# A decoder stack on one core: in the ternary stage ScalarE scales and shifts the last four weight chunks, and VectorE clips them after its last chunk of z

## The reference, cut to what matters

```
scale = 1.0 / clip(mean(|w|), 1e-5)                 # one number for a whole weight
wq    = clip(round(w * scale), -1, 1) / scale
gate  = act_quant(x) @ wq_gate.T ;  up = act_quant(x) @ wq_up.T
inter = silu(gate) * up                             # 2048 wide, called z in the kernel
out   = act_quant(fwht(inter)) @ wq_down.T          # fwht: Walsh-Hadamard over 2048
x     = layernorm(x + out)
```

## Time and profile before

| | us |
|---|---|
| median of 3 runs | 1766.6 |
| lowest and highest of them | 1761.59, 1771.72 |
| the profiled execution's own time | 1760.69 |
| its span, from the first to the last instruction | 1758.8 |

### The profile page before, as it was taken

The page is one execution under the profiler, slowest core; times in us unless marked ns, Lnnn a source line. Parts: engine busy times, 40 slices in busy tenths (PEclk is TensorE's granted clock), DMA queues, the critical chain, the costliest instruction groups (busy, mean ns, idle before and its releaser), DMA issues. The chain is left out here.

```text
span 1758.8 us, 26394 instructions
## 1 busy us (share of the span) xinstructions
PE 1591.5 (90%) x8780; PEld 1121.4 (64%) x8812; DVE 1296.5 (74%) x2354; ACT 936.4 (53%) x1932; POOL 690.9 (39%) x646
## 2 busy tenths in 40 slices
PE   7999998999867899999889999999898989999995
PEld 5788875555525556566666566565566767677774
DVE  6466656666888899997687585784849999767574
ACT  3221226776665566666566465473634555555542
POOL 5034265776522332323332222322132235555553
PEclk9999999999988999999999999999999999999998
DMA  6200018533020000003312121121233100000000
GB/s 213 75 1 24 1 49 234 173 97 97 26 96 1 1 1 1 1 1 104 89 55 73 37 73 55 55 73 37 86 99 93 46 10 1 1 25 12 13 24 24
DMA packets 66849, 95.72 MB, mean 54 GB/s; under 512 B 12176, under 2 KB 28688, under 8 KB 66716
## 3 DMA queue, kind: packets, MB, share of 16 engines
q1 hardware_dynamic: 58460, 80.40, 15.0%
q0 software_dynamic: 6144, 12.60, 2.8%
q10 hardware_dynamic: 2112, 1.05, 0.2%
HBM read 56.25 MB, written 4.19 MB: 34 GB/s over the span
## 5 line engine op out<-in xcount | busy, mean ns | idle before, releaser
L2948 PE MATMUL bank<-fp_xT,fp_weights_values 128*128 128x512 f32 x704 | 187.1, 404 | 11.6 <-DVE fp_gate L2851 9.8
L1783 ACT ACTIVATE causal_probs<-bank,causal_neg 128x512 f32<-128x512 f32 (+3 forms) x256 | 134.1, 530 | 106.0 <-DVE causal_neg L1853 70.8
L2948 PEld LDWEIGHTS bank<-fp_xT,fp_weights_values 128*128 128x128 f32 x704 | 129.7, 190 | 57.1 <-DVE fp_gate L2851 18.0
L2975 PE MATMUL bank<-fp_wd,fp_hT 128*128 128x512 f32 x528 | 133.8, 394 | 4.6 <-DVE X L2873 3.4
L2860 DVE SCALAR_TENSOR_TENSOR fp_up<-bank,fp_weights_scales,fp_up 128x512 f32<-128x512 f32 x132 | 99.1, 751 | 44.5 <-ACT fp_up L2758 37.0
L820 DVE TENSOR_REDUCE heads_neg<-bank 128x1 f32<-128x512 f32 x128 | 86.7, 679 | 57.7 <-PE bank L869 57.6
L782 ACT ACTIVATE heads_probs<-bank,heads_neg 128x512 f32<-128x512 f32 x128 | 88.1, 689 | 77.1 <-DVE heads_neg L820 77.1
L1126 POOL DMA_DIRECT2D causal_qS<-causal_qk x96 | 48.4, 511 | 202.3 <-DVE causal_qk L1118 202.2
L1185 POOL TENSOR_TENSOR ternary_z<-ternary_z 128x1024 f32<-128x1024 f32 x16 | 37.7, 2354 | 206.1 <-DVE ternary_z L1376 206.1
L2975 PEld LDWEIGHTS bank<-fp_wd,fp_hT 128*128 128x128 f32 x528 | 98.5, 188 | 28.9 <-issue 6.6
L1511 PE MATMUL bank<-weights_raw,ternary_qT 128*128 128x512 bf16 x433 | 104.7, 388 | 4.6 <-DVE ternary_z L1376 2.6
(11 more groups left out here) (266 smaller groups left out, 4128.2 us busy)
## 6 DMA issues: line engine op xcount, KB each, us to landing
pairs_xd<-X SPq DMA_DIRECT2D x64, 128.0 KB, 2.7
pairs_cd<-in_ctx SPq DMA_DIRECT2D x64, 128.0 KB, 2.8
causal_qS<-causal_qk SPq DMA_DIRECT2D x96, 64.0 KB, 2.8
causal_qS<-causal_qk POOLq DMA_DIRECT2D x96, 64.0 KB, 2.5
causal_kS<-causal_qk SPq DMA_DIRECT2D x96, 64.0 KB, 2.7
causal_kS<-causal_qk POOLq DMA_DIRECT2D x96, 64.0 KB, 2.5
X<-in_x SPq DMA_DIRECT2D x4, 1024.0 KB, 7.8
heads_cT<-in_ctxT SPq DMA_DIRECT2D x4, 1024.0 KB, 6.1
```

The costliest lines, as they stand in the source:

```text
L1783: act.activation(probs_of(i)[:, h + one], view[:, one], ACT.Exp, bias=neg[:, G % 2, at:at + 1], accum_out=total[:, G % 2, at:at + 1]).then ...
L2948: last = pe.matmul(banks[4 + g][:], values[:, g, n % NI, of], xT[:, part, g], start=part == 0, stop=part == 1)
L2975: last = pe.matmul(banks[t][:], hT[:, n % SLOTS, a, t * P:(t + 1) * P], wd[:, c, i], start=i == 0 and k == 0, stop=i == NI - 1 and k == 2)
```

## The change

In steps 2 and 3 the shift of the two chunks moves from VectorE's queue to ScalarE's. It is a new helper, `shift_by_act`, which does the same arithmetic, from the chunk to the same place, in one ScalarE instruction: the rate is its scale operand (one number per partition) and ROUND its bias. ScalarE issues it behind silus(t, 3) and ahead of `keep_q`, with a wait for the rate and one for the shift before it. VectorE's `round_weights` becomes `clip` alone, and this stands behind z_chunk(t, 3) instead of ahead of it. Chunks 0 to 7, all other steps, all transfers and all sizes stay.

```diff
+    def shift_by_act(self, act, n):
+        act.wait_ge(self.rated, 2)
+        act.wait_ge(self.shifted, n)
+        act.activation(self.chunks[n], self.chunks[n], ACT.Copy, scale=self.rate[:, n // 4:n // 4 + 1],
+                       bias=ROUND).then_inc(self.shifted, 1)
@@ ScalarE's step
                 silus(t, 3)
+                if t in (2, 3):
+                    for n in (2 * t + 4, 2 * t + 5):
+                        weights.shift_by_act(act, n)
                 if tile(t + 1) and t >= 0:
@@ VectorE's step
                     weights.means(dve, slice(2, 3), banks[4][:, 0:1], 2)
+                z_chunk(t, 3)
                 if t in (2, 3):
                     for n in (2 * t + 4, 2 * t + 5):
-                        round_weights(n)
-                z_chunk(t, 3)
+                        weights.clip(dve, n)
                 peaks(t - 2)
```

## The result

| | before | changed |
|---|---|---|
| median us (20 runs each) | 1765.78 | 1775.58 |
| lowest run | 1760.74 | 1767.37 |
| ratio to before, 95% interval | | 1.0039 [1.0023, 1.0055] |
| span of the profiled execution, us | 1758.8 | 1777.3 |
| from z(2,2) to the first z of step 4 in it | 584.33 - 539.08 = 45.25 | 591.28 - 539.62 = 51.66 |

z(2,2), VectorE's third z of tile 2, starts at 539.08 and 539.62, ahead of all that the change touches; these 0.5 us arose ahead of the stage (a matching instruction stands at 300.21 and 300.68 already). One run of each twenty (1868.62 and 1862.83) was in a slower state; it counts in the medians and not in the ratio. So steps 2 and 3 cost **6.4 us** more, where +3.3 was forecast, and in these two profiles the part behind the stage took another 10.9 us more.

A forecast was written before the change was run, and what follows sets the result against it. Bound: shift_y(0)'s start in step 2 and the last keep in step 3. Terms: +2.1 (step 2) + 1.2 (step 3) + 0 (clock) = +3.3 us on the median 1766.6, giving 1769.9; range 1761 to 1777.

The forecast's parts named there:

- What bounds the steps: Steps 2 and 3: shift_y(0)'s start sets the end of step 2, the last keep that of step 3.
- ScalarE's queue: Step 2: two ScalarE shifts of 2.00 us and the keeps behind them make shift_y 1.58 us late by ScalarE's queue.
- The clips beside GpSimd: Step 2: clips meeting GpSimd's butterflies cost 1.23 to 1.88 us each, 1.88 taken; step 2 +2.1 us.
- Step 3: Last keep ends at 576.42 instead of 575.19, +1.2 us; clip contention hidden by 0.4 us.
- The clock: TensorE's granted clock in steps 2 and 3: -2.1 to +2.8 us, taken as 0.
- Behind step 3 nobody idles, so it is carried to the end: Behind step 3: the +3.3 us from steps 2 and 3 reaches the end of the kernel unchanged.
- Table loads: Rival, steps 2 and 3: ScalarE's added instruction costs four table loads of 1.28 us; +8.4 us, 1775.0; chance 0.03.
- VectorE decides and the shifts vanish: Rival, steps 2 and 3: VectorE's work decides and its shifts simply vanish; -5.2 us, 1761.4; chance 0.06.
- The slower rival: Steps 2 and 3: ScalarE's queue becomes the whole path, down(0) at the lower clock; +10.2 us, 1776.8; chance 0.07.
- "Same" and not "slower": Whole kernel: a measurement tells some 0.5%, 9 us, from no change; same 0.91, slower 0.07, faster 0.02.

The follow-up runs named there:

- e3: Changed kernel with GpSimd's butterflies in steps 2 and 3 waiting until both clips are done; median 1764.7 us, ratio to before 0.9994.
- e2: Changed kernel with VectorE's clips ahead of z_chunk(t, 3) again, ScalarE still shifting; median 1766.5 us, ratio to before 1.0007.
- e7: Kernel before plus a pure delay: VectorE reduces y(0) once more, into an unused place, ahead of its peaks; median 1765.4 us, ratio 0.9994.
- e8: Kernel before with step 3's rounding moved ahead of z of the third chunk, ScalarE's two keeps ahead of keep_q; median 1765.8 us, ratio 0.9985.
- e11: The same version as e8, run again against the kernel before; median 1763.6 us, ratio 0.9997.
- e9: Changed kernel plus one 128x512 VectorE reduce, 0.6 us, into an unused place ahead of peaks(0); median 1769.8 us, ratio to before 1.0032.
- e4: The changed kernel again without an edit; median 1774.9 us, ratio to before 1.0047.
- e12: The changed kernel a third time without an edit; median 1770.0 us, ratio to before 1.0047.
- e5: Changed kernel with GpSimd's two butterfly instructions of tiles 2 and 3 cut into four each; median 1764.9 us, ratio to before 0.9996.

## Why the prediction was right in its range and short in its main term

The measured 1775.6 lies in the stated 1761 to 1777, but only by the widening for the spread of runs: the terms' own bounds ended at +6.1 us and 1773, and both the +6.4 at the steps and the median lie over them. In that the hit is luck.

- **What bounds the steps: right.** shift_y(0)'s start and the last keep of step 3 set the two ends. In the changed kernel the same two moved, and step 4 with them.
- **ScalarE's queue: right.** Two shifts took 4.09 and 4.08 us for 4.04 worked out. Without contention shift_y would come 1.58 late by the sum; in e3, where only that is left, step 2 came out 1.63 us longer (from z(2,2) to the first z of step 3, 18.75 against 17.12).
- **The clips beside GpSimd: the term that was mis-sized.** The step was "so a clip costs 1.23 to 1.88, and I take 1.88, since the row above is just this meeting". The meeting was the right one, the bound was not: in rows 8 and 9 the VectorE instruction asked at 457.24, behind the start of a GpSimd instruction that ran only to 456.76 + 1.28 = 458.04. It ended at 459.12, 1.08 behind that end, and in the changed kernel the two clips of step 2 end 1.08 and 1.09 behind GpSimd's ends. Another meeting in the trace of before has the same distance at another price:

```profile
464.68 1.59 DVE L615 TENSOR_SCALAR weights_raw<-weights_raw 128x2048 f32<-128x2048 f32 x1
```

```profile
462.65 2.53 POOL L663 TENSOR_TENSOR pairs_cL<-pairs_cd,pairs_cH 128x1024 fp32r<-128x1024 f32 x1
```

  The clip ends at 466.27, 1.09 us behind GpSimd's 465.18, and took 1.59 because it asked only 0.50 us before that end. GpSimd's instructions in steps 2 and 3 are 2.36 long, so what is left of one can be 2.3. The 1.88 was read as a slowdown of the clip, bounded by itself, when it was the remainder of the other's instruction and 1.1 us more. Measured: 2.57 and 3.37. Step 2 cost 4.1 instead of 2.1.
- **Step 3: the same error, and a cover that went.** "Clip 11 starts at 572.20 and ends by 574.08 even at 1.88, ahead of keep 11, so the contention is hidden by 0.4 us here." With 5.87 us for both, keep 11 waited 1.38 us for it and ended 2.75 us later, counted from SiLU(3,3) (582.03 - 571.62 against 575.19 - 567.53), where 1.2 was forecast. TensorE gave 0.5 back ahead of that SiLU and took 0.1 behind the keep, and step 3 cost 2.3. Where the cover held (e2, e3), it cost 0.6 and 0.7; e7, where nothing in step 3 is changed, has 0.7 too, so some tenths of these are the clock's.
- **The clock: right in sign on both sides, its bound above too small.** In the changed kernel turn_y took 1.76 for 1.89 and VectorE waited 0.48 for the SiLU of step 3 instead of 1.01, so 0.5 us were won; down(0) lost 0.1. In e3 turn_y ran in 1.07 us and VectorE did not wait for the SiLU of step 3, so the 1.01 us were won; down(0) took 5.16 instead of 4.53, and 0.6 was lost. The bound below was right, down(0) took 3.40 in e8; the bound above, 4.53 + 1.1 = 5.6, was not: 6.13 in e11 and 6.17 in e9, with the same work. TensorE in e3:

```profile
558.93 1.07 PE L1532 MATMUL bank<-ternary_eye,ternary_yq 128*128 128x128 bf16 x16 [0.36 <-DVE ternary_yq L1434]
...
578.36 5.16 PE L1566 MATMUL bank<-ternary_w_down,ternary_yT 128*128 128x512 bf16 x15 [8.38 <-issue]
```

- **"Behind step 3 nobody idles, so it is carried to the end": right for the work, incomplete for the time.** The ternary stage carried it. Behind it the tail differs between the fourteen profiles by up to 12 us, more than the change is worth. The lowest runs are no sure guide either: +6.6 for +6.4 in the changed kernel's twenty and +2.3 for +2.4 in e3, but +8.9 and +8.5 for the same +6.4 and +6.6 in e4 and e12, and +2.9 for +0.3 in e5. Runs sorted by their granted clock follow it best.
- **Rivals.** Table loads: none appeared in steps 2 and 3. VectorE decides and the shifts vanish: no, it waited. The slower rival named 1776.8, near the 1775.6 measured, and that is luck: at the steps it named +10.2 for the 6.4 measured, and its mechanism was wrong. ScalarE was not the whole path, it waited for VectorE, and VectorE for GpSimd.
- **"Same" and not "slower"** holds by the measure stated, 1.0039 being under 0.5%, though the interval reaches over it. The measure itself was too coarse: with twenty runs each the interval, 1.0023 to 1.0055, leaves no doubt that the kernel is slower. In numbers: 1769.9 was forecast, 1775.6 measured, 1761 to 1777 the range.

## What to carry to other kernels

When an instruction of VectorE moves in time, look up which GpSimd instructions it will now meet, and price a meeting by the whole remaining length of the other engine's instruction, not by a ratio seen elsewhere. If the trace has such meetings, line up the ends of the two instructions and not their lengths: here the distance of the ends was the same 1.1 us each time while the lengths went from 1.59 to 3.37. Freeing an engine of work buys nothing where its next instruction then waits for the engine that took the work over; and what the earlier z triggered on GpSimd made VectorE's four clips 7.0 us longer, more than the 5.2 us of shifts that had left it. And where whole executions scatter by more than the effect, measure the effect at its place, from an instruction ahead of the change to one behind it, and compare whole executions of like granted clock.

## What the runs showed of the hardware

A VectorE tensor_scalar on 128x2048 f32 in SBUF and a GpSimd tensor_tensor on 128x1024 f32 in SBUF did not run side by side in any profile here, shift and clip alike. VectorE's, when it came second, ended 1.08 to 1.09 us behind GpSimd's end; GpSimd's ended 2.2 us behind VectorE's (3.31 to 3.34 long for 2.36); and when both had something queued they took turns. VectorE's tensor_reduce on the same kind of tile kept its 2.28 us beside GpSimd's butterflies in the kernel before (the peaks from 550.14, GpSimd from 550.30). GpSimd's work in eight instructions took 7.5 us (e5) where two took 4.7, which was free here, since it had until the next step.
